# An attention and feed-forward block on one core: the gather at the beginning becomes a selection with a one-hot matrix, and the idle products are left out

## What is computed

```
w = cond_weights[itok_B_0_30]                    # (32, 32, 32), one matrix for each sequence
c = einsum('bct,bcd->bdt', x, w)                 # each sequence's tokens are mixed by its own matrix
q, k, v = c @ wq.T, c @ wk.T, c @ wv.T           # 32 heads of 16
q, k = rope(q), rope(k)
x1 = x + softmax(causal(q k^T / 4)) v @ wo.T     # attention within each sequence
h = x1 @ W.T + 2 * (top-2 gated LoRA of 8 experts of rank 16, a bias of 5 for expert itok_B_0_7)
out = x1 + unpermute(gelu(permute(h) @ up) @ down)   # 16 heads of 32, inner size 128
```

## Time and profile before

| | |
|---|---|
| median of three runs | 217.81 us (217.02 to 218.19) |
| the profiled execution's own time | 216.94 us |
| its span, from the first to the last instruction | 215.1 us |
| PE busy | 201.6 us (94%) |
| DVE, POOL, ACT busy | 147.3, 122.4, 114.2 us |

### The profile page before, as it was taken

How to read it: one execution, slowest core, us unless ns; L and a number is a source line. 1 busy time by engine, 2 the same in 40 slices (tenths; PEclk the granted TensorE clock), 3 DMA queues, 4 the chain that set the end, 5 groups by cost and what they waited for, 6 DMA issues and landing times.

```text
span 215.1 us, 5966 instructions
## 1 busy us (share of the span) xinstructions
PE 201.6 (94%) x2536; PEld 175.2 (81%) x2536; DVE 147.3 (68%) x283; ACT 114.2 (53%) x189; POOL 122.4 (57%) x96
## 2 busy tenths in 40 slices
PE   4999698699999999999999999999999999798993
PEld 4989675598878999988679899986788987688863
DVE  2368799899488978775646877836769886158223
ACT  2173173692271536439983337289865866533460
POOL 6628996959786201487985201978997344425000
PEclk9999999999999999999999999999999999999999
DMA  6699983300001050000026320000044300134002
GB/s 202 194 375 292 337 282 101 91 11 3 0 3 53 0 186 12 5 0 5 0 27 76 101 97 0 3 0 3 0 52 94 56 5 3 10 38 52 0 3 98
DMA packets 10858, 15.43 MB, mean 72 GB/s; under 512 B 2288, under 2 KB 6544, under 8 KB 10832
## 3 DMA queue, kind: packets, MB, share of 16 engines
q1 hardware_dynamic: 8384, 11.99, 16.8%
q0 software_dynamic: 2160, 3.05, 8.7%
q10 hardware_dynamic: 288, 0.01, 0.1%
HBM read 11.25 MB, written 3.80 MB: 70 GB/s over the span
## 4 chain that ended last, share of the span: by engine, by line
PE 86%; DVE 7%; issue 3%; ACT 2%; DMA 1%
PE ps_A L593 12%; PE ps_A L595 11%; PE ps_A L594 11%; PE ps_F L593 8%; PE ps_F L594 7%; PE ps_F L595 7%; PE ps_S L699 6%; PE ps_F L789 4%; PE ps_A L625 4%; PE ps_S L804 3%; PE ps_S L825 3%; PE ps_S L677 3%; PE ps_A L699 1%; PE ps_A L817 1%; DMA cst<-constants 1%
## 5 line engine op out<-in xcount | busy, mean ns | idle before, releaser
L974 ACT ACTIVATE pbd<-pr 32x512 f32<-32x512 f32 x56 | 35.3, 630 | 5.9 <-DVE pr L1311 5.2
L535 POOL TENSOR_TENSOR pr<-pr,small 128x512 f32<-128x512 f32 x16 | 17.6, 1111 | 35.5 <-DVE small L1305 35.4
L474 POOL TENSOR_TENSOR rot<-rot,cst 128x512 f32<-128x512 f32 x14 | 19.1, 1361 | 15.0 <-DVE rot L1261 14.8
L515 POOL DMA_INDIRECT out<-y,row_at x12 | 19.8, 1646 | 11.3 <-ACT y L974 8.8
L1062 ACT ACTIVATE act<-ps_F 128x512 f32<-128x512 f32 x32 | 16.5, 603 | 11.2 <-PE ps_F L789 11.2
L1283 DVE TENSOR_TENSOR kbd<-kr,cst 128x512 f32<-128x512 f32 x16 | 20.7, 1320 | 2.4 <-POOL kr L478 2.4
L489 POOL TENSOR_TENSOR kbd<-kr,cst 128x512 f32<-128x512 f32 x16 | 20.1, 1283 | 2.1 <-PE ps_F L602 2.0
L593 PE MATMUL ps_A<-xc,wqT 128*128 128x256 f32 x64 | 18.2, 285 | 1.7 <-DVE xc L1229 1.7
L1018 ACT ACTIVATE pr<-pr 128x512 f32<-128x512 f32 x16 | 10.0, 631 | 16.4 <-DVE pr L1297 16.2
L593 PE MATMUL ps_A<-xc,wkT 128*128 128x256 f32 x64 | 18.3, 286 | 0.0
L594 PE MATMUL ps_A<-xc,wkT 128*128 128x256 f32 x64 | 17.9, 279 | 0.0
(11 more groups left out here) (187 smaller groups left out, 614.7 us busy)
## 6 DMA issues: line engine op xcount, KB each, us to landing
xs<-in_x SPq DMA_DIRECT2D x4, 512.0 KB, 6.3
xt<-in_xT SPq DMA_DIRECT2D x4, 512.0 KB, 3.3
out<-xt SPq DMA_DIRECT2D x3, 512.0 KB, 3.0
pbd<-in_L_attn_wq SPq DMA_DIRECT2D x2, 512.0 KB, 4.4
act<-in_L_attn_wk SPq DMA_DIRECT2D x1, 1024.0 KB, 6.2
act<-in_L_attn_wv SPq DMA_DIRECT2D x1, 1024.0 KB, 8.6
act<-in_L_attn_wo SPq DMA_DIRECT2D x1, 1024.0 KB, 10.0
out<-xt SPq DMA_DIRECT2D x2, 256.0 KB, 2.2
```

The lines of the kernel that those rows point to most:

```text
L474: pool.tensor_tensor(rv, rv, con("sin").unsqueeze(1).to_broadcast([P, 2 * N // T, T]), ALU.mult).then_inc(rot_sin, 1)
L515: pool.indirect_dma_start(out=out, out_offset=bass.IndirectOffsetOnAxis(ap=row_at[:, g, c:c + 1], axis=0), in_=y[:, c, :], in_offset=None, ...
L535: pool.tensor_tensor(pr[:, i, :, :], pr[:, i, :, :], mx[:, i, :].unsqueeze(2).to_broadcast([P, NH // 2, T]), ALU.mult).then_inc(normed, 1)
L974: return sc.activation(dst, src, ACT.Copy)
```

## The change

The constants' tensor now carries the conditional weights too, 256 more columns laid out so that partition 32r + s holds a quarter r of matrix s. DVE makes a one-hot matrix from the sequence numbers (one `is_equal` over 128 columns), PE selects the matrices of all sequences by 16 small matmuls (contraction over 32, output of 32 partitions by 256 columns), DVE turns the four results (four transpositions of 128x256) into `wsel`, and the block matrices of all groups are made from it. The two row gathers, the gather of whole matrices, its way through DRAM and all 22 idle products are gone; nothing takes the idle products' place. x of group 0 is loaded from ACT's queue, wq in three pieces.

Its other parts: the first group's cond goes out in four half banks, Q(0) runs over both halves together, chunk by chunk, behind four separate splits of wq (`first_q`); Q(0) and K(0) lie in ring F. V(0) follows K(0) at once, all of `prep_w2` moves behind scores(0, 0), and the last of them, `prep_w2(3)`, behind Q(1). Three of the four k_blocks of tile 1 go to ACT. `w2b`'s four buffers now are two in xt, one in y and one in the third of `vz`; this third is zeroed by POOL after `prep_w2(3)` and ahead of `wo_los`.

```
@@ POOL
-            pool.wait_ge(idx_ready, 1)
-            cond_rows(0)
-            cond_rows(1)
+            pool.memset(pbd[:, 1, 0:HC, :, :], 0.0).then_inc(pbd_zero, 1)
             pool.wait_ge(d_ids, 16)
-            cond_seqs()
-            pool.memset(pbd[:, 1, :, :, :], 0.0).then_inc(pbd_zero, 1)
-            pool.wait_ge(d_permc, 16)
-            pool.wait_ge(d_w["wk"], 16)
+            pool.wait_ge(d_wq2, 16)
             perm_rows()
             for i in range(3):
                 rope(0, i)
-            for t in range(GT):
-                for c in range(2):
-                    k_blocks(0, t, c)
-            wait_w(pool, "wq")
+            k_blocks(0, 0, 0)
+            k_blocks(0, 0, 1)
+            k_blocks(0, 1, 0)
+            wait_w(pool, "wq", KC)
             pool.memset(pbd[:, 0, :, :, :], 0.0).then_inc(pbd_zero, 1)
+            pool.memset(pbd[:, 1, HC:2 * HC, :, :], 0.0).then_inc(pbd_zero, 1)
             for g in range(G):
...
                     norm(g, 0)
                     norm(g, 1)
                 if g == 0:
+                    wait_full(pool, prep("w2", KC - 1))
+                    pool.memset(vz[:, 2, :, :], 0.0).then_inc(vz_zero, 1)
                     wo_los()
@@ PE
+            def select(r):
+                it = Fi("sel", r)
+                rows = slice(T * r, T * r + T)
+                for j in range(BT):
+                    at = slice(T * j, T * j + T)
+                    last = pe.matmul(bank(it)[at, 0:SC * T], onehot[rows, at], wst[rows, :],
+                                     start=True, stop=True, skip_group_check=True)
+                last.then_inc(s_full(it), 1)
...
             pe.wait_ge(d_cst, 16)
-            idle_products(16)
-            cond(0, 0)
-            cond(0, 1)
-            idle_products(6)
-            qk(0, "wq", Q, 0)
-            qk(0, "wq", Q, 1)
-            qk(0, "wk", K_, 0)
-            qk(0, "wk", K_, 1)
+            pe.wait_ge(onehot_ready, 1)
+            for r in range(BT):
+                select(r)
+            first_conds()
+            first_q()
+            qk(0, "wk", 0)
+            qk(0, "wk", 1)
+            v(0, 0)
+            v(0, 1)
+            scores(0, 0)
             pe.wait_ge(d_w["w2b"], 16 * KC)
-            for k in range(KC - 1):
-                prep_w2(k)
-            prep_b()
-            wait_w(pe, "wv")
-            v(0, 0)
-            scores(0, 0)
-            prep_w2(KC - 1)
-            v(0, 1)
+            prep_w2(0)
+            prep_w2(1)
             cond(1, 0)
             cond(1, 1)
+            prep_w2(2)
+            prep_b()
             scores(0, 1)
...
                 if g == 0:
+                    prep_w2(KC - 1)
                     pv(0, 0, 0)
@@ ACT
             w_his("wv", raw["wv"], WT["wv"], (d_w["wv"], None))
             blocks(1)
-            for k in range(KC - 1):
-                turned_hi(prep("w2", k), WT["w2"][:, 0, k, :])
-            turned_hi(prep("b"), bT[:, 0, :])
             w_his("wo", raw["wo"], WT["wo"], (d_w["wo"], None))
+            w_his("a", raw_a, aT, (d_w["a"],))
             v_out(0, 0)
-            turned_hi(prep("w2", KC - 1), WT["w2"][:, 0, KC - 1, :])
+            for c in range(1, KC):
+                k_blocks(c)
+            v_out(0, 1)
+            turned_hi(prep("w2", 0), WT["w2"][:, 0, 0, :])
             exp(0, 0)
-            v_out(0, 1)
-            exp(0, 1)
             cond_hi(1, 0)
             cond_hi(1, 1)
-            w_his("a", raw_a, aT, (d_w["a"],))
+            exp(0, 1)
@@ DVE, first group
-                    w2_los(2)
                     max_shift(0, 2)
+                    rope(1, 0)
                     max_shift(0, 3)
-                    split_lo(prep("b"), bT[:, 0, :], bT[:, 1, :], prep_hi, KC)
-                    rope(1, 0)
+                    rope(1, 1)
                     sums(0, 2)
                     sums(0, 3)
-                    w2_los(3)
-                    rope(1, 1)
+                    w2_los(1)
                     turn(g, 2)
                     turn(g, 3)
+                    w2_los(2)
                     rope(1, 2)
+                    split_lo(prep("b"), bT[:, 0, :], bT[:, 1, :], prep_hi, KC)
+                    w2_los(3)
                     blocks(2)
                     rope(1, 3)
```

More of the change, by code:

```diff
@@ L78, in constants, with build @@
     return c
-def build(nc, x, xT, who, wcond, wq, wk, wv, wo, w2b, wr, wa, up, down, perm, consts, cols, rows, out):
+def build(nc, x, xT, who, wq, wk, wv, wo, w2b, wr, wa, up, down, consts, cols, out):
     ctx = ExitStack()
@@ L611, in prep_b, with first_conds @@
                 last.then_inc(s_full(it), 1)
+            def select(r):
[6 more added lines that the diff above has]
+                last.then_inc(s_full(it), 1)
+            def first_conds():
+                pe.wait_ge(d_x[0], 16)
+                pe.wait_ge(wbd_ready, 1)
+                for c in range(KC):
+                    for t in range(GT):
+                        for r in range(2):
+                            it = first_cond(c // 2, r)
+                            rows = slice(P // 2 * r, P // 2 * r + P // 2)
+                            at = P * (c % 2) + P // 2 * t
+                            last = pe.matmul(bank(it)[:, at:at + P // 2], xs[rows, 0, t, P * c:P * c + P],
+                                             wbd[rows, t, :, :], start=True, stop=True, skip_group_check=True)
+                            if t == GT - 1 and c % 2:
+                                last.then_inc(s_full(it), 1)
             def cond(g, t):
                 pe.wait_ge(d_x[g], 16)
-                pe.wait_ge(wbd_ready, g + 2 if g else t + 1)
+                pe.wait_ge(wbd_ready, g + 1)
                 its = [A(g, COND + r) for r in range(2)]
@@ L628, in cond, with first_q, qk @@
                             last.then_inc(s_full(it), 1)
-            def qk(g, name, first, i):
+            def first_q():
+                its = [QK(0, i) for i in range(2)]
+                for it in its:
+                    wait_free(pe, it)
+                W = WT["wq"]
+                for k in range(KC):
+                    wait_w(pe, "wq", k + 1)
+                    if k % 2 == 0:
+                        for r in range(2):
+                            wait_read(pe, first_cond(k // 2, r))
+                    for i, it in enumerate(its):
+                        for h in range(2):
+                            c = 2 * i + h
+                            last = mm3(bank(it)[:, N * h:N * h + N],
+                                       W[:, 0, k, P * c:P * c + P], W[:, 1, k, P * c:P * c + P],
+                                       xc[:, 0, k, :], xc[:, 1, k, :], h == 0 and k == 0, h == 1 and k == KC - 1,
+                                       skip=True)
+                        if k == KC - 1:
+                            last.then_inc(s_full(it), 1)
+            def qk(g, name, i):
                 W = WT[name]
@@ L1442, in _ @@
                                ).then_inc(mask_ready, 1)
-            ve.wait_ge(d_permc, 16)
+            for r in range(BT):
+                turn_selected(r)
+            blocks(0)
             step(ve.tensor_copy(permf, permc[:, :]))
@@ L1614 @@
         give(f"in_{name}", given[name])
-    give("constants", constants())
+    give("constants", np.concatenate([constants(), given["L0_cond_weights"]], axis=1))
     give("columns", np.broadcast_to(np.arange(D, dtype=np.float32), (P, D)))
-    args.append(nc.dram_tensor("rows", (B, T * T), F32, kind="Internal").ap())
     args.append(nc.dram_tensor("out_0", (G * D, N), F32, kind="ExternalOutput").ap())
```

259 lines of the change are left out of this document (142 added, 117 removed).

## The result

The changed kernel takes 220.94 us (median of four runs, 220.37 to 222.77); the kernel before, on the same chip, takes 217.71 us (217.02 to 218.19). The ratio is 1.0156, with a 95% interval of 1.0095 to 1.0217: slower, by about 3.2 us (the interval lies above 1 and reaches to both sides of 1.02).

What follows compares the result with a forecast made beforehand. PE, busy 94% of the span, was taken as the bound. Q(1) 6.2 us earlier but V(1) 3.1 later gave 216.94 + 3.1 = 220.0; half of 0.9 added for the median made 220.4, range 216.9 to 224.3.

Steps and rivals of the forecast that it cites:

- The likeliest case: Whole kernel: Q(1) starts between 35 and 38 us, V(1) is delayed, time 218.5 to 222 us; chance 0.47.
- the rival of the clock: PE's gaps before K(1)'s second half and V(1): clock drops to 1.2 GHz, up to 2.5 us more, about 222.6; chance 0.2.
- The beginning up to Q(0)'s start: Start of kernel: mixing from 7.8 us, cond(0) at half clock, Q(0) starts at 11.7, about 1.8 us earlier.
- Q(0) and the clock: Q(0) on PE: clock rises 5 us after 7.8 us, 1.1 us at half clock, loss 0.6; ends at 18.1.
- POOL's wait: Before the memset of `vz`'s third: POOL waits for `prep_w2(3)` behind Q(1), standing still for over 3 us.
- DVE's order: Rope of Q(1)'s second half goes ahead of two sums and waits for POOL; POOL's norms start 2.45 us later.
- V(1): V(1)'s start on PE: at 59.8 us, 3.1 us later than before, though Q(1) starts 6.2 earlier.
- The two gaps: PE before K(1)'s second half and V(1): idle 48.1 to 52.6 and 55.5 to 59.8 us, together 8.8 us.
- POOL's instructions were no shorter: Rival, POOL between 43 and 58 us: instructions shorten when DVE stands still, up to 5.7 us, 214.3; faster side's chance 0.13.
- its bounds: Selection at the start of the kernel: 16 small matmuls on PE take 0.5 to 2.2 us.
- ACT was not late: Rival, emptying V(0): ACT waits for Wo and A, cond(1) and all behind come 1 to 2 us later, 221.5; chance 0.06.
- no gain survived: Rival: faster beginning and K(0) rope, Q(1) starts at 33.7, gain survives in part, 217.1 to 217.9 us; chance 0.14.

Runs made afterwards that it cites:

- e8_change_again: The changed kernel run once more, unaltered, on another chip; 222.01 us, ratio 1.0180 to the kernel before.
- e1_pool: Against the changed kernel: POOL makes Wo's low part ahead of its wait on `prep_w2(3)` and the memset; 220.34 us, ratio 1.0041 to the kernel before.
- e2_dve: Against the changed kernel: DVE makes the sums ahead of the rope of Q(1)'s second half; 220.55 us, ratio 1.0048 to the kernel before.
- e3_both: Changed kernel with both moves, e1_pool's on POOL and e2_dve's on DVE; 216.41 us, ratio 0.9861 to the kernel before.
- e12_wohalf_again: Against e3_both: POOL makes half of Wo's low part ahead of the first norms; repeat on another chip, 213.65 us, ratio 0.9818 to the kernel before.
- e9_order: Against e12_wohalf_again: POOL's wait goes behind the rope of Q(1)'s first half, ACT's exponentials among the probability blocks; 212.80 us, ratio 0.9783 to the kernel before.
- e10_order_idle6: Against e9_order: six idle products, five between selection and mixing, one behind the mixing; 210.97 us, ratio 0.9680 to the kernel before.
- e4_idle8: Against the changed kernel: eight idle products, two before the selection, five between it and cond(0), one after; 223.25 us, ratio 1.0159 to the kernel before.

## Why the prediction was right

The forecast was 220.4 us, the result 220.94. The likeliest case is the one that came, with its mechanism; the rival of the clock came beside it. Step by step:

- **The beginning up to Q(0)'s start**: right. 7.8 us for the mixing was 7.91, 0.12 us a record was 0.12, 11.7 for Q(0) was 11.52.
- **Q(0) and the clock**: the step that failed in its size. "1.1 us of Q(0) are at the half clock, a loss of 0.6": Q(0) took 7.9 us (11.52 to 19.45) and not 5.85, a loss of 2.1. The forecast had put the rise five us behind the first mixing product, by the earlier trace rows; it came about eight us behind it. Q(0) ended 1.35 us late by this term, and Q(1) started at 38.41 us, not at 36.6. (In e8_change_again, the same kernel, the rise came at 15 us and Q(1) started at 37.86.) The other terms on the way nearly held, among them the 6.5 us of K(0)'s rope with its contention (26.08 to 32.58 us); the last wait in front of scores(0, 0) was 0.59 us for POOL's blocks of K, not DVE's.
- **POOL's wait**: right. 3.77 us in front of the memset, where "over 3" was forecast.
- **DVE's order**: right. The shuffle was ended by POOL, 2.39 us of wait in front of the norms, 2.45 forecast. e1_pool and e2_dve show each of the two orders for itself, e3_both that together they are all of the loss.
- **V(1)**: 22.90 us behind Q(1), 23.2 forecast. With Q(1) 1.8 late it came at 61.31, 59.8 forecast.
- **The two gaps**: right in the sum, not one by one. 4.52 and 2.56 us of idle time, 7.1 in all; the second is shorter by the 1.6 us that K(1)'s half clock took, which the forecast didn't count. With it the two are 8.7 us against 8.8.
- **The rival of the clock**: its condition was met, against its chance of 0.2. The clock fell in the gaps in both profiles of the change, and the mean granted clock was 0.974 to 0.985 in all its runs (in the kernel before 1.000 as profiled, 0.977 to 1.000 in its other runs). Its price at V(1) was 0 and 1.3 us in the two profiles, since it came back for a while under K(1); the run at 0.974 leaves room for the forecast's 2.5. The rule of the Trainium skill's page "TensorE: Matmul & The Clock Gate", section "What's actually happening", that idleness brings back the half clock, was the better guide here; the gaps of 4.52 us here and 3.95 in e1_pool agree with it.
- **The rivals that did not come**: POOL's instructions were no shorter when DVE stood: Wo's low part 4.74 us beside an idle DVE, 4.73 before. The selection was in the middle of its bounds. ACT was not late: PE has no wait between scores(0, 0) and Q(1). And no gain survived, since V(1) started at 61.31 us.

By its own terms the sum would have given 216.94 + 4.6 = 221.5 us with V(1) where it was, and 222.8 with the clock: the profiled execution's 222.77. The median is lower. e8_change_again's profile, at 220.88 us, shows how it can be: the clock comes up earlier at the beginning and is at full when V(1) starts; the other runs of the result have no profile. That the forecast lies 0.5 us from the median is in part luck: Q(0)'s clock, and with it Q(1)'s start, was mis-sized by 1.3 to 1.8 us, which comes through in full, and the clock's price in the gaps was left out; the 0.45 us added for the median, and a median execution in which both errors are small, made up for most of that. The profiled execution lies 2.4 us above the forecast.

## What to carry to other kernels

An earlier start is worth what is left of it at the next place where PE has to wait for another engine, and a PE that looks fully busy hides how near that place is. Here two lines on engines other than PE, a wait ahead of Wo's low part and a rope ahead of two sums, turned 4.4 us of lead into 4.6 of delay, and exchanging them made the same beginning a gain. Look at each engine's list for what is queued behind a new wait, before looking at the stage that was changed.

Idle products paid where PE waits anyway, behind the first useful work: six gave 1.8 us in the kernel with its orders mended. Eight, two of them ahead of the selection, gave nothing in the change as it was. The two cases differ both in the place of the products and in the room of the chain behind, and no run separates the two causes; what is seen is that the selection began 0.54 us late behind the two, and that DVE came to its first rope at 18.08 us with the eight and at 16.42 with the six.

## What the runs showed of the hardware

- The clock's rise at the beginning comes at a different time in executions of the same beginning. PE reached 10 or 11 matmul records a us from 14 us in e12_wohalf_again and e9_order, from 15 in e8_change_again, after 16 in the change's own profile; Q(0)'s last product then started anywhere from 17.98 to 19.47 us and Q(1) from 37.06 to 38.55. An edit worth less than 1.5 us there can't be read from one profile each.
- With PE busy on idle products from 5.66 us, the second bank of the mixing took 1.06 us for 16 records in e10_order_idle6; in e9_order, without them, 1.95 us.
- The gaps of 3.95 us in e1_pool and 4.52 us in the change were followed by half clock; so were shorter ones of 2.56 us in the change and 2.42 in e4_idle8, which came soon after the clock had returned from half. Those of 1.55 us in e3_both and e8_change_again were not, nor the one of 2.1 us in the kernel before. No run separates the length of a gap from what went before it.
- The same split of 1024 columns on DVE took 1.2 us beside an idle POOL and 2.34 beside a working one, and taking it away from POOL made the next pair of instructions meet, a product of 0.67 us taking 1.81: what one place gained, the other lost.
- A stretch with the same instructions, 148.3 to 148.5 us in every profile on the other chips, took 149.6 to 149.9 in the four on chip 1. The cause is not shown.
